# Graph attention, first row group: x transposes and relu ahead of the second features, GpSimd's normalises ahead of its scaling, inverse deviations behind the statistics

## The reference

```python
h = jnp.maximum(_layernorm(x, axis=-1), 0.0)      # x: 8192 x 128, float32
Wh = h @ W                                        # W: 128 x 128
f1, f2 = Wh @ a[:128, 0], Wh @ a[128:, 0]
e = leaky_relu(f1[:, None] + f2[None, :], 0.2)    # 8192 x 8192
e = jnp.where(adj == 0, -inf, e)                  # adj: 8192 x 8192, int32
x = x + softmax(e, axis=1) @ Wh
```

## Time and profile before

| | |
|---|---|
| median of 3 runs | 810.79 us (809.84 to 810.98) |
| the profiled execution's own time | 810.9 us |
| its span in the trace | 809.2 us (1.7 us lie around it) |
| PE busy | 785.9 us, 97% of the span |
| PEld, DVE, ACT, POOL busy | 718.5, 740.8, 483.5, 419.2 us |
| 256 adjacency loads of 256 KB, issue to landing | 7.4 us, median |
| mean granted TensorE clock, share of full speed | 0.997 |

### The profile page before, as it was taken

How to read it: one execution, slowest core, us unless ns; L and a number is a source line. 1 busy time by engine, 2 the same in 40 slices (tenths; PEclk the granted TensorE clock), 3 DMA queues, 4 the chain that set the end, 5 groups by cost and what they waited for, 6 DMA issues and landing times.

```text
span 809.2 us, 22590 instructions
## 1 busy us (share of the span) xinstructions
PE 785.9 (97%) x8969; PEld 718.5 (89%) x8969; DVE 740.8 (92%) x1189; ACT 483.5 (60%) x777; POOL 419.2 (52%) x621
## 2 busy tenths in 40 slices
PE   5899999999999999999999999999999999999997
PEld 4778799999999999999999999999999999999986
DVE  6997899999999999999999999999999999999996
ACT  6788865655655565565555556565555656555542
POOL 7687755544545554454545445454544545454320
PEclk9999999999999999999999999999999999999999
DMA  9998899999999999999999999999999999998200
GB/s 172 169 106 85 79 108 114 110 96 107 85 101 95 97 91 88 110 85 101 91 100 91 87 110 86 101 88 104 90 88 107 89 100 86 106 90 87 27 14 17
DMA packets 48321, 75.99 MB, mean 94 GB/s; under 512 B 4768, under 2 KB 13600, under 8 KB 48288
## 3 DMA queue, kind: packets, MB, share of 16 engines
q0 software_dynamic: 43008, 67.13, 87.8%
q1 hardware_dynamic: 4864, 8.39, 3.1%
q10 hardware_dynamic: 416, 0.07, 0.0%
HBM read 272.70 MB, written 4.19 MB: 342 GB/s over the span
## 4 chain that ended last, share of the span: by engine, by line
PE 90%; issue 3%; ACT 2%; DVE 2%; POOL 2%; DMA 1%; ACTq 0%; POOLq 0%; DVEq 0%
PE acc L392 53%; PE acc L396 27%; PE stage L382 7%; PE stage L365 2%; DVE wt_ring L811 1%; PE stage L373 1%; ACT ht L542 1%; DMA a_sb<-in_L_gnn_a_dram 1%; PE stage L349 1%; POOL xn L248 0%; ACT wh L549 0%; POOL tmp L267 0%; POOL masks L224 0%; POOL masks L239 0%; ACT tmp L562 0%
## 5 line engine op out<-in xcount | busy, mean ns | idle before, releaser
L811 DVE SCALAR_TENSOR_TENSOR wt_ring<-stage,packed,marks 128x512 f32<-128x512 f32 x1024 | 697.6, 743 | 54.1 <-PE acc L396 42.5
L392 PE MATMUL acc<-pairs,wt_ring 128*128 128x258 f16 x4096 | 718.9, 274 | 2.4 <-DVE pairs L801 1.3
L396 PE MATMUL acc<-pairs,wt_ring 128*128 128x129 f16 x4096 | 697.4, 219 | 0.0
L392 PEld LDWEIGHTS acc<-pairs,wt_ring 128*128 128x128 f16 x4096 | 396.0, 97 | 56.7 <-DVE pairs L801 2.2
L571 ACT ACTIVATE marks<-stage 128x1024 uint16<-128x1024 uint8 x256 | 262.0, 1023 | 290.5 <-PE stage L382 289.3
L396 PEld LDWEIGHTS acc<-pairs,wt_ring 128*128 128x128 f16 x4096 | 399.5, 98 | 2.5
L239 POOL TENSOR_TENSOR masks<-masks 128x256 int32<-128x256 int32 x256 | 184.2, 734 | 240.4 <-ACT masks L591 239.6
L214 POOL DMA_DIRECT2D masks<-in_adj_dram x240 | 130.3, 545 | 99.5 <-PE stage L382 77.5
L591 ACT ACTIVATE masks<-masks 128x512 uint16<-128x512 uint16 x256 | 158.9, 622 | 0.5 <-DMA masks<-in_adj_dram 0.5
L382 PE MATMUL stage<-ident,masks 128*128 128x128 f32 x512 | 99.2, 276 | 1.5 <-POOL masks L239 0.9
L382 PEld LDWEIGHTS stage<-ident,masks 128*128 128x128 f32 x512 | 53.0, 141 | 6.4 <-issue 2.8
(11 more groups left out here) (60 smaller groups left out, 143.9 us busy)
## 6 DMA issues: line engine op xcount, KB each, us to landing
masks<-in_adj_dram POOLq DMA_DIRECT2D x256, 256.0 KB, 7.4
out_dram<-xm SPq DMA_DIRECT2D x15, 256.0 KB, 7.2
xm<-in_x_dram SPq DMA_DIRECT2D x1, 1536.0 KB, 13.4
xm<-in_x_dram SPq DMA_DIRECT2D x1, 1024.0 KB, 10.5
xm<-in_x_dram SPq DMA_DIRECT2D x1, 768.0 KB, 5.8
xm<-in_x_dram SPq DMA_DIRECT2D x1, 512.0 KB, 7.6
xm<-in_x_dram SPq DMA_DIRECT2D x1, 256.0 KB, 3.2
out_dram<-xm SPq DMA_DIRECT2D x4, 64.0 KB, 2.6
```

Of the source, the lines that this page charges most:

```text
L392: return nc.tensor.matmul(acc[:, r, 0:2 * E1], wtv[:, w, r, 1, :], pairv[:, t, :, 0:E1], start=st, stop=end)
L396: return nc.tensor.matmul(acc[:, r, 0:E1], wtv[:, w, r, 0, :], pairv[:, t, 0, 0:E1], start=False, stop=False)
L811: nc.vector.scalar_tensor_tensor(out=wtq[:, t % NW], in0=e_row, scalar=packed[:, t, 1:2], in1=edges[:, k], op0=ALU.max, op1=ALU.mult).then ...
```

## The change

`order of one step`: on PE the x transposes move from behind P1 to behind P0 and F0, so they stand ahead of P1; F1 stays behind P1. On ACT relu(b+3) moves ahead of keep(b+2, 1), the exponentials and unpack. On POOL normalise(b+4) moves ahead of scaled(b+2), except in steps 2 and 6 (and 0), where it stays behind. On DVE the inverses of steps 2 and 6 move behind pack and statistics; that of step 0 stays. No instruction is added or taken away, and no buffer or semaphore changes.

```diff
@@ gpsimd, for b in range(UN) @@
                 for u in MIXES.get(b, (b + 2,)):
                     mix(u)
+
+                if b + 4 < NQ and b not in ROOTS:
+                    normalise(b + 4)
                 if b + 2 < NQ:
                     scaled(b + 2)
-                if b + 4 < NQ:
+                if b + 4 < NQ and b in ROOTS:
                     normalise(b + 4)
@@ tensor @@
                     if b + 2 < NQ and k == 0:
                         features(b + 2, 0)
-                    if b + 3 < NQ and k == 1:
+                    if b + 3 < NQ and k == 0:
                         x_transposes(b + 3)
                     if b + 2 < NQ and k == 1:
                         features(b + 2, 1)
@@ scalar @@
                 if b in ROOTS:
                     root(ROOTS[b])
+                if b + 3 < NQ:
+                    relu(b + 3)
                 if b + 2 < NQ:
                     keep(b + 2, 1)
                     exponentials(b + 2)
                 if b + 2 < UN:
                     unpack(b + 2, b + 2, first=True)
-                if b + 3 < NQ:
-                    relu(b + 3)
                 if b + 4 < NQ:
                     normalise(b + 4)
@@ vector @@
-                if b in ROOTS:
+                if b == 0:
                     inverses(ROOTS[b])
-                if b == 0:
                     next_group(1)
                 if b + 2 < NQ:
                     pack(b + 2)
                 for g in STATS.get(b, ()):
                     statistics(g)
+                if b in ROOTS and b > 0:
+                    inverses(ROOTS[b])
                 if b in LAST:
                     moments(LAST[b])
```

## The result

| | before | changed |
|---|---|---|
| median | 810.38 us (20 runs, 809.84 to 810.98) | 811.55 us (20 runs, 810.31 to 813.06) |
| profiled execution, its span | 810.9, 809.2 | 811.13, 809.5 |
| ratio changed to before, 95% interval | | 1.0015 (1.0009 to 1.0021) |

2.4 us faster was forecast; it is 1.2 us slower.

The account below looks back on a forecast made before the run. PE's exit from the first row group counts: DVE bounds steps 1 to 6, a loop of waits steps 7 to 13. Terms 0, -0.1, 2.35 and 0.1 give 2.4 us off 810.9: 808.5, range 806.6 to 811.4.

Parts of the forecast that it names:

- The loop through relu: Steps 8 to 12: waits through F0, X, F1, keep 1, unpack and relu set the pace; opened, 4.80 falls to 4.33 us.
- 2.35 and 0.1: Terms of the sum: 2.35 us won in steps 8 to 12, 0.1 in the last steps with unpack no longer late.
- Rival B: Steps 8 to 12: late scaled delays keep 0 and F1, steps fall only to about 4.6; 809.9 us, chance 0.18.
- Rival A: Stalls before X(3) and X(7) don't hold, PE enters step 8 0.8 to 1.3 early; about 807.0 us, chance 0.18.
- I take 0 for steps 1 to 6: Early steps, DVE the bound: no net gain or loss; bounds +0.84 kept and -0.67.
- step 7: -0.1: X(7) waits for normalise(10) with P1 now behind it, so PE enters step 8 about 0.1 us late.
- P1 uncovered: Lower bound for steps 1 to 6: P1 no longer runs in the wait ahead of X, once, -0.67 us.
- Rival C: New PE idle before X(7) or X(3) brings the 1.2 GHz clock once, 1.6 us lost; 810.1 us, chance 0.10.
- Rival D: Steps 1, 3, 4 and 5: low_part waits behind the normalises, 1.31 us a step; 813.7 us, chance 0.12.
- The term of the sum that let low_part wait for one normalise of three: Port wait on DVE: 0.44 us inside DVE's slack of 0.6 in steps 8 to 12, 0 in earlier steps.
- POOL: I take 0: Normalise ahead of scaled: fills the wait for the exponentials, may delay scaled and keep 0; no gain or loss.
- DVE's saved port wait: Step 2: inverses moved behind statistics miss scaled, 0.84 us won, which drains in step 3 behind POOL's normalise.

Follow-up runs that it names:

- e8: The changed kernel with 14 more identity transposes put into PE's wait ahead of each of X(3) and X(7); median 810.81 us.
- e9: The kernel before with X early from step 8, relu early and normalise ahead of scaled from step 7, inverses as before; 808.94 us.
- e7: The kernel before with only POOL's move, normalise ahead of scaled; 811.72 us, ratio 1.0017.
- e1: The kernel before with only the PE and ACT moves (X ahead of P1, relu ahead of keep 1) in all steps; 814.44 us.
- e6: The kernel before with only DVE's move, the inverses of steps 2 and 6 behind pack and statistics; 811.82 us.
- e12: The kernel before with relu early and POOL's order moved in all steps, X behind P1 and inverses as before; 809.93 us.

## Why the prediction was wrong

**Right: where it counts, and the late steps.** Only the exit of the first row group moved. The loop through relu was the one that bound steps 8 to 12, and the new step is 4.34 (weights(12) to weights(13), 78.16 to 82.50) for 4.33 forecast. 2.45 us came in where 2.35 and 0.1 stood in the sum, but that the two agree is luck: the five steps from weights(9) to weights(14) gave 1.98, and the one behind them (4.40 before, 3.93 after) 0.47 where 0.1 was taken.

**Rival B** (F1 waits for keep 0, steps of 4.6) is part of that. It had a chance of 0.18 as a price on all five steps and comes true in one of the changed kernel: weights(10) to weights(11) takes 4.57 us. There scaled stands behind the normalises, high_part behind scaled, keep 0 behind high_part and F1(9) behind keep 0:

```profile
70.09 0.64 ACT L623 ACTIVATE pairs<-tmp 128x516 f16<-128x516 f32 x1 [0.56 <-POOL tmp L267]
...
71.05 0.52 PEld L368 LDWEIGHTS stage<-wx,ht 128*128 128x128 f32 x4 [0.24 <-ACT wh L552]
```

**Rival A** (the stalls don't hold) fell: X(7) starts at 61.03 us, later than before and not well before 58.

**Wrong: "I take 0 for steps 1 to 6" and "step 7: -0.1".** They cost 2.73, by the starts of the weights: +0.78 up to weights(4) (0.54 of it the spell that only the profile of before has), -2.43 in the step to weights(5), -0.77 in the step to weights(7) (low_part 1.48), +0.39 and -0.78 around step 7, with +0.08 between. The pattern had been seen: X ahead of P1, P1 uncovered, priced at 0.67 for step 3. Three things were left out of it. The early pack that lets F0(3) go makes PE idle longer (1.77 us), where before F0 waited for the same pack (1.05 us). P1 and F1 then hold the exponentials, which DVE, full until then, waits for 2.38 us: a stall of PE was costed at PE's slack when its heir was the bound engine. And the clock falls, which is 1.35 of the 2.43 by e8.

**Rival C** (a slow clock behind the stall) had a chance of 0.10 and is in the profile: 2.99 for 1.56 us, 1.4 lost where 1.6 was priced. It is also what spreads the runs: with a mean clock of 0.998 the change took 810.3 to 810.8, at 0.996 810.3 to 811.9, at 0.994 812.3 to 813.1. What decides how many spells an execution has stays open; X(7), with as long an idle ahead of it, has none in the profile. The same kind of spell from 26 to 30 us in the kernel before cost less, 0.55, DVE being the bound: weights(2) to (3) is 5.63 with it and 5.08 in e9 without.

**Rival D** (low_part behind GpSimd) was half right: 0.6 in step 2 and 0.8 in each of steps 5 and 7. But the holder was scaled (in step 5 pushed there by the normalises), or a mix and then one normalise at most, and never three normalises in a row; in e7 they gave way themselves. The term of the sum that let low_part wait for one normalise of three named the wrong instruction, and the 0 that it stood at in the early steps was too low. The Trainium skill (SBUF — State Buffer, "Who interferes with whom") calls the port pair that DVE shares with GpSimd an exclusive lock and says that either side can be the one blocked. The 1.74 us of three normalises beside the low_part of 62.09, and the 1.92 in e7, agree.

**Also wrong: "POOL: I take 0".** Normalise ahead of scaled opens the second loop in the late steps, and it has a price in the early ones, 1.3 by e7. Had it been weighed as a step that the early X needs, e1's 5.27 would have been on the page, and with it that X early is the dangerous edit. And DVE's saved port wait could not come through while normalise and mix on POOL hung on the same inverses; that part of the text held (e6), but the edit was a loss and not a zero.

## What to carry to other kernels

An in-order engine's instruction should move forward only if its inputs move too: list every step on the way to each input, for the ordinary steps and for those with extra work, and what is queued behind it. When a loop of waits is cut, write out the next loop before counting the gain: here it ran through GpSimd, at 5.27 with the transpose early, 4.6 with it late, 4.3 in most steps once GpSimd's order followed. And reorder only the steps that the loop binds: bound to the late steps, two of the four moves gave 2.1 us, while all four everywhere lost 1.2.

## What was not expected of the hardware

- A one-input tensor_scalar of 128 x 24 float32 on DVE (moments) took 0.80 us in place of 0.22 beside a GpSimd tensor_tensor, and a low_part 1.92 in e12, 0.69 alone: scaled lay beside it from 29.36 to 30.40 and then the issue of a load up to 31.16; what held it after scaled isn't shown.
- Ahead of X(3) TensorE waited 1.16 us for a low_part and then 1.77 us, and about 3 us at the 1.2 GHz level followed (granted clock 0.54 and 0.60 from 38 to 40 and 40 to 42 us). Ahead of X(7) it waited 1.71 us and the clock stayed at 1.00. With 28 useless transposes in the two gaps the median was about 0.7 us lower, with overlapping intervals.
